# Cross-attention: one of sixteen additions of probabilities per key block on GpSimd instead of VectorE

## The reference

```python
q = (x @ Wq).reshape(B, N, 16, 32).transpose(0, 2, 1, 3)      # x is layer-normed
k = (context @ Wk).reshape(B, M, 16, 32).transpose(0, 2, 1, 3)
v = (context @ Wv).reshape(B, M, 16, 32).transpose(0, 2, 1, 3)
attn = jax.nn.softmax(q @ k.T * 32 ** -0.5, axis=-1)          # masked; M = 8192 keys
out = (attn @ v).transpose(0, 2, 1, 3).reshape(B, N, 512) @ Wo
```

## Time and profile before

| | us |
|---|---|
| median of 3 runs | 1930.38 (1928.66 to 1931.12) |
| the profiled execution's own time | 1917.37 |
| its span | 1915.6 |
| busy: TensorE, VectorE, ScalarE, GpSimd | 1841.6, 1706.8, 1457.6, 45.9 |
| exponentials (line 1733), 1024 of them | 1096.9 |
| additions of probabilities (line 1881), 496 of them | 1135.0 |

### The profile page before, as it was taken

How to read it: one execution, slowest core, us unless ns; L and a number is a source line. 1 busy time by engine, 2 the same in 40 slices (tenths; PEclk the granted TensorE clock), 3 DMA queues, 4 the chain that set the end, 5 groups by cost and what they waited for, 6 DMA issues and landing times.

```text
span 1915.6 us, 56880 instructions
## 1 busy us (share of the span) xinstructions
PE 1841.6 (96%) x24652; PEld 812.1 (42%) x24652; DVE 1706.8 (89%) x1530; ACT 1457.6 (76%) x1660; POOL 45.9 (2%) x57
## 2 busy tenths in 40 slices
PE   8999999999999998999999999999998989998895
PEld 4444444444444443334444444444442445556431
DVE  6899999999999999979999999999998588788655
ACT  2699999999988987869998888989987465555121
POOL 2000000000000000000000000000000000001103
PEclk9999999999999999999999999999999999999998
DMA  8333333333333333322333333333333000005795
GB/s 262 119 95 100 105 98 101 106 106 106 101 95 98 99 84 101 111 68 78 90 101 84 84 90 90 96 90 96 89 79 122 24 1 1 2 1 207 245 307 165
DMA packets 113773, 196.21 MB, mean 102 GB/s; under 512 B 10352, under 2 KB 64624, under 8 KB 113520
## 3 DMA queue, kind: packets, MB, share of 16 engines
q1 hardware_dynamic: 110528, 183.33, 32.6%
q0 software_dynamic: 2560, 8.39, 1.3%
q10 hardware_dynamic: 432, 0.79, 0.1%
HBM read 109.63 MB, written 50.33 MB: 84 GB/s over the span
## 4 chain that ended last, share of the span: by engine, by line
PE 40%; DVE 40%; issue 15%; ACT 3%; DMA 1%; POOL 1%; DVEq 0%; POOLq 0%; SPq 0%; ACTq 0%
DVE dacc L1881 31%; PE ps L1217 8%; PE ps L1464 7%; PE ps L1116 4%; PE ps L1113 4%; PE ps L1306 3%; PE ps L1244 2%; DVE wsm L1824 2%; DVE wsm L2203 2%; PE ps L1346 2%; PE ps L1201 2%; PE ps L1269 2%; PE ps L1153 1%; PE ps L1301 1%; PE ps L1315 1%
## 5 line engine op out<-in xcount | busy, mean ns | idle before, releaser
L1733 ACT ACTIVATE pt<-ps,bias 128x1024 f32<-128x1024 f32 x1024 | 1096.9, 1114 | 182.0 <-PE ps L1464 99.2
L1881 DVE TENSOR_TENSOR dacc<-dacc,pt 128x2048 f32<-128x2048 f32 x496 | 1135.0, 2288 | 42.9 <-ACT pt L1733 16.2
L1464 PE MATMUL ps<-qst,kst 128*32 128x512 f16 x8192 | 620.7, 380 | 12.1 <-ACT pt L1733 10.1
L1217 PE MATMUL ps<-pt,vt 128*32 128x512 f32 x4096 | 485.1, 592 | 0.0
L1464 PEld LDWEIGHTS ps<-qst,kst 128*32 128x32 f16 x8192 | 211.6, 97 | 367.1 <-issue 153.4
L1116 PE MATMUL ps<-wsm 128*32 128x512 f16 x4608 | 314.9, 380 | 0.0
L1113 PE MATMUL ps<-wsm 128*32 128x512 f16 x4464 | 305.7, 379 | 0.0
L1217 PEld LDWEIGHTS ps<-pt,vt 128*32 128x32 f32 x4096 | 123.9, 110 | 211.0 <-issue 145.7
L1116 PEld LDWEIGHTS ps<-wsm 128*32 128x32 f16 x4608 | 125.4, 97 | 125.7 <-issue 3.2
L1113 PEld LDWEIGHTS ps<-wsm 128*32 128x32 f16 x4464 | 120.8, 97 | 121.0 <-issue 2.0
L1824 DVE SCALAR_TENSOR_TENSOR wsm<-ps,wsm 128x512 f16<-128x512 f32 x126 | 86.0, 683 | 8.1 <-ACT wsm L1549 8.0
(11 more groups left out here) (229 smaller groups left out, 1231.2 us busy)
## 6 DMA issues: line engine op xcount, KB each, us to landing
kst<-kscr SPq DMA_DIRECT2D x132, 256.0 KB, 3.5
kscr<-wsm SPq DMA_DIRECT2D x126, 256.0 KB, 3.5
kst<-kst SPq DMA_DIRECT2D x124, 256.0 KB, 3.4
wsm<-in_ctx SPq DMA_DIRECT2D x31, 768.0 KB, 5.3
wx<-in_gate SPq DMA_DIRECT2D x10, 512.0 KB, 8.2
wx<-in_fc SPq DMA_DIRECT2D x10, 512.0 KB, 9.5
wx<-in_proj SPq DMA_DIRECT2D x10, 512.0 KB, 9.2
qst<-qscr SPq DMA_DIRECT2D x32, 128.0 KB, 3.2
```

The source lines that it names most:

```text
L1217: p = e.matmul(ps[32 * h:32 * h + 32, 4 + n % 2, :], vt[:, kb % 2, ch, c:c + 32], pt[:, (2 * i + h // 2) % 6, h % 2, :], start=ch == 0, st ...
L1464: p = e.matmul(ps[r:r + 32, 2 * half + h2, :], kst[:, kb % 2, h, ch * 128 + r:ch * 128 + r + 32], qst[:, h, :], start=True, stop=True)
L1733: e.activation(pt[:, (2 * i + half) % 6], ps[:, 2 * half:2 * half + 2, :], ACT.Exp, bias=bias[:, 4 * kb + ch:4 * kb + ch + 1], scale=SCORE ...
L1881: e.tensor_tensor(own_heads, own_heads, probs, ALU.add).then_inc(S["add"], 1)
```

## The change

In each block from 1 to 30, the addition of step 11 (third group, fourth chunk) leaves VectorE's program and stands in GpSimd's. GpSimd waits for both exponentials of that step and for VectorE's addition of the step before. It raises a new semaphore `padd`. ScalarE waits for it, too, before it writes the same slot of the ring, three steps later (step 14); VectorE waits for it before it next adds to the same part of `dacc`, thirteen steps later (step 8 of the next block); `finish` waits for it on TensorE. The thirty instructions stand in GpSimd's program behind its start-up work and ahead of its wait for the flag. `added` counts without the moved steps.

```diff
+ON_POOL = [i for i in range(16, STEPS - 16) if i % 16 == 11]
 def added(i):
-    return i + 1 - sum(x <= i for x in ON_PE)
+    return i + 1 - sum(x <= i for x in ON_PE + ON_POOL)
+
+def pooled(i):
+    return sum(x <= i for x in ON_POOL)
...
             i.then_inc(S["split"], 1)
+            for i in ON_POOL:
+                g = i // 4 % 4
+                e.wait_ge(S["ex"], 2 * i + 2)
+                e.wait_ge(S["add"], added(i - 1))
+                e.tensor_tensor(dacc[:, 4 * g:4 * g + 4, :], dacc[:, 4 * g:4 * g + 4, :],
+                                pt[:, 2 * i % 6:2 * i % 6 + 2].rearrange("p a b c -> p (a b) c"),
+                                ALU.add).then_inc(S["padd"], 1)
             choose(e, "pool")
...
                 e.wait_ge(S["add"], added(256 * b + 240 + 4 * g + 3))
+                e.wait_ge(S["padd"], pooled(256 * b + 240 + 4 * g + 3))
...
                         e.wait_ge(S["add"], added(i - 3))
+                        if i - 3 in ON_POOL:
+                            e.wait_ge(S["padd"], pooled(i - 3))
...
                     e.wait_ge(S["add"], added(i - 1))
+                    if i - 13 in ON_POOL:
+                        e.wait_ge(S["padd"], pooled(i - 13))
                     e.tensor_tensor(own_heads, own_heads, probs, ALU.add).then_inc(S["add"], 1)
...
-                if i not in ON_PE:
+                if i not in ON_PE and i not in ON_POOL:
                     adds(i)
```

More of the change, by code:

```diff
@@ L704 @@
  pool dve act hi0 chi lo0 wsplit split var root norm n1 xt xTc qry qlo unit khi klo vev maxs max1 bias esl
- sc ex add av oac fin dnc dnx okr att prj x2 flagm flag
+ sc ex add padd av oac fin dnc dnx okr att prj x2 flagm flag
  xn turn xTh xTs whi wlo relu p01 abs amp p23 p4 sv ms mroot msr phi tabs sin cos polar qkT QT KT
```

## The result

Median of four runs 1988.62 us (1986.55 to 1989.91) against 1930.66 us before: ratio 1.0305, 95% interval 1.0291 to 1.0318. The change costs 58 us. The forecast was 1998 with 1932 to 2034, slower at 0.80.

What follows compares the result with a forecast made beforehand. VectorE (43.57 us a block) barely slower than TensorE (43.09) was taken as the bound. +59.0 for 27 blocks, +6 for three others, +3 statistics gave +68; on 1917.4 plus 13.0 carried along, 1998 us, range 1932 to 2034.

Steps and rivals of the forecast that it cites:

- The two paces: Steady key blocks before the change: TensorE's own pace is 43.09 us a block, VectorE's 43.57, only 0.48 us slower.
- What the addition takes on GpSimd: Step 11's 128x2048 addition on GpSimd: between 4.21 and 4.63 us, taken as 4.4.
- VectorE waits: Steady blocks: VectorE stands still while GpSimd adds, for 4.4 us, making its block 45.7 us.
- Variant 1: The forecast case: VectorE waits while GpSimd adds, 41.28 + 4.4 = 45.7 us a block, +68 us in all; chance 0.40.
- The sum of the 27 blocks: Blocks 1 to 14 and 18 to 30 at 45.7 us: 1233.9 against 1174.9 us, +59.0.
- the statistics: VectorE's statistics in four of the second batch's blocks, 4 x 0.69 us, come on top of 45.7 again: +3 us.
- VectorE's block in the prediction: 16 x 2.29 + 4 x 0.68 + 3 x 0.68 us, four `k_low` and small gaps; 43.57 - 2.29 = 41.28 after.
- Variant 2: Steady blocks: GpSimd waits and VectorE doesn't; 46.7 us a block, +92 us, 2022 in all; chance 0.26.
- Blocks 15 to 17: Three blocks where VectorE partly had reserve: between 0 and 3.6 us each, taken as 2, +6 in all.
- The lag: VectorE falls back 0.48 us per short block before the change; block 1 was nevertheless charged 45.7 us like the rest.
- The waits: ScalarE waits for GpSimd at step 14, 30 times, 1 to 4 us each; TensorE loses 2.8 us at step 15.
- no contention: Steady blocks: GpSimd's addition hides, TensorE sets 43.09 us a block; 12 to 20 us faster, about 1914; chance 0.15.

Runs made afterwards that it cites:

- At step 3: The change with GpSimd's thirty additions taken from step 3 of each block instead of step 11: 1978.95 us, ratio 1.0262 against the kernel before.
- the multiplication by a constant: Kernel before, VectorE keeping all additions, plus an unrelated one-input GpSimd multiplication of 128x1536 in 28 blocks, nobody waiting except VectorE thirteen steps later: 2011.30 us, one execution.
- the run in four pieces: The change as made, but GpSimd's addition cut into four instructions of 128x512: 2036.96 us, ratio 1.0557 against the kernel before.

## Why the prediction was right

- **The two paces.** 43.09 for TensorE and 43.57 for VectorE hold: without the addition every steady block is at 43.09.
- **What the addition takes on GpSimd.** Forecast 4.4 us, bounds 4.21 and 4.63. At step 3, where nothing holds it at its start, it took 4.54 to 4.58 in 29 of 30 blocks; 4.89 at step 11, where L2221 holds it. The price that the Trainium skill gives in "GPSIMD Engine Reference" (3.1), 4497 ns, is 1 to 2% under the 4.54 to 4.58.
- **VectorE waits.** Variant 1 said 41.28 + 4.4 = 45.7 us a block; measured 45.54, as 41.28 + 4.37 = 45.65 less 0.1 of gaps. The mechanism was right: VectorE's addition ends 2.15 us after GpSimd's in all but two of the thirty blocks, so it is stopped to the end and nothing is shared. It is the whole-instruction rule of the Trainium skill, "SBUF — State Buffer", "Who interferes with whom", and the trace agrees in both directions, in block 30 with GpSimd as the one that waits. Only behind the multiplication by a constant did VectorE go on 0.9 us before GpSimd's recorded end.
- **The sum of the 27 blocks** agrees in part by luck. With the statistics it said +62, and they took +58.7. Blocks 2 to 14 took 45.54 each, 0.16 less than assumed. Block 1 took 43.17, 2.5 less. Blocks 18 to 30 took 46.04 on average, 0.34 more, the statistics among it and block 30, which the forecast had charged like the rest and which by itself took 5.4 us more than before.
- **VectorE's block in the prediction** was listed as the durations of its instructions "and small gaps". These durations add up to 44.1 us, more than the 43.57, since many instructions start up to 0.08 us before the recorded end of the one ahead. The forecast used only the difference of one addition, so its result doesn't suffer.

- **Variant 2** gave VectorE a right of way that it doesn't have. It rested on L1806, whose counterpart on GpSimd was perhaps through with reading (above).
- **Blocks 15 to 17.** +6 forecast, +1.8 measured, the term that was most off. Block 15, which VectorE sets, cost 3.35; block 16 gained 1.50; block 17, where VectorE has room, stayed at 52.49. Of the 10 us between 1998 and 1988.6, 4.2 are this term, 3.3 the 27 blocks with the statistics, and 2.6 lie between the blocks of the two profiles (+60.6) and the timed runs (+58.0).
- **The lag.** Block 1 still took 43.17 us, since GpSimd's addition fell partly into VectorE's idle time ahead of step 12; from block 2 on VectorE was late and paid in full. The forecast had charged it like the rest.
- **The waits.** ScalarE was to wait for GpSimd 30 times, 1 to 4 us each; it waited 27 times, 65.9 us. TensorE was to lose 2.8 us at step 15; it waited 1.83, and had the room, because VectorE's own time was the longer. That the two paths lie so close, as the prediction said (45.7 and 45.9), the run in four pieces bears out: there VectorE has room, and TensorE's wait sets the block.
- **The rival "no contention"** is confirmed as a number, 12 to 20 us (17 measured with the additions left out or only written), and wrong as an outcome.

## What to carry over

Work that GpSimd takes from VectorE counts against VectorE for nearly as long as GpSimd's instruction reads SBUF, if VectorE's next instruction has two inputs in SBUF; here 2.29 us were saved for 4.37 us lost. Ask of an offload what VectorE will be doing in that very window: the same kind of move gains once it is short and lies beside instructions that read PSUM. What waits for GpSimd's end counts as well, once VectorE no longer sets the pace. And price the removal on its own first: here VectorE was over TensorE by 0.48 us in 43.57, so 17 us was all there was to win.

## What was not expected of the hardware

- GpSimd's multiplication by a constant is slow, 4.37 us for 128x1536 against 1.77 for a copy (both include up to 0.46 us behind L2212; one execution each), and holds VectorE's addition for 3.01 us.
- Cutting GpSimd's instruction in four doesn't soften the conflict but has both engines take turns at waiting: 7.8 us for 4.9. VectorE then loses less, yet the kernel is slower still (1.0557 against 1.0305), because ScalarE and TensorE wait for the last piece, and in many blocks the granted clock falls to 0.96 or 0.93.
